# A selective scan whose gate y*silu(z) is made by VectorE out of PSUM, with five shared products a chunk in place of four

## The reference

```python
def step(h, inp):                       # over the 1024 tokens of a sequence
    ut, dt_, bt, ct = inp
    dA = jnp.exp(dt_[..., None] * A)
    dBu = ((dt_ * ut).reshape(b, nCh, ch, 1) * bt[:, :, None, :]).reshape(b, din, ds)
    h = dA * h + dBu
    y = (h.reshape(b, nCh, ch, ds) * ct[:, :, None, :]).sum(-1).reshape(b, din)
    return (h, y)
...
y = ys.transpose(1, 0, 2)
y = (y + u * D) * jax.nn.silu(z)
return y @ Wout.T + bout
```

## Time and profile before

| | |
|---|---|
| median of 3 runs | 901.68 us (898.56 to 904.07) |
| profiled execution | 903.63 us |
| its span, first to last instruction | 901.8 us |
| busy: PE, DVE, POOL, ACT | 738.7, 642.1, 512.7, 322.8 us |
| mean granted TensorE clock | 0.934 |

### The profile page before, as it was taken

One profiled execution on the slowest core, in us unless ns is written; L12 is line 12 of the kernel. 1 busy time (PEld: TensorE's weight loads), 2 busy tenths in 40 slices (PEclk: granted clock), 3 DMA queues, 4 the chain that ended last, 5 costly groups with the idle time before them and its releaser, 6 DMA issues.

```text
span 901.8 us, 10200 instructions
## 1 busy us (share of the span) xinstructions
PE 738.7 (82%) x2240; PEld 364.4 (40%) x2241; DVE 642.1 (71%) x876; ACT 322.8 (36%) x359; POOL 512.7 (57%) x266
## 2 busy tenths in 40 slices
PE   5899896878777787879678787895179999999994
PEld 3434342323232232323222232584136666666663
DVE  4467687999999999999989799486324444444442
ACT  1567675444353544444344344111021111111110
POOL 0013232889989999999988899546502222222222
PEclk9899997999999999999999899997579999999998
DMA  9354525454545554454556555296312222222220
GB/s 273 95 135 140 175 116 177 162 189 170 184 168 162 188 170 183 174 176 172 154 181 204 188 196 197 95 365 212 128 39 42 42 44 46 46 45 42 40 37 0
DMA packets 59059, 125.19 MB, mean 139 GB/s; under 512 B 9818, under 2 KB 30618, under 8 KB 58908
## 3 DMA queue, kind: packets, MB, share of 16 engines
q1 hardware_dynamic: 48676, 116.12, 39.6%
q0 software_dynamic: 7152, 8.48, 5.5%
q10 hardware_dynamic: 3208, 0.34, 0.3%
HBM read 98.01 MB, written 23.63 MB: 135 GB/s over the span
## 4 chain that ended last, share of the span: by engine, by line
PE 48%; DMA 14%; DVE 13%; POOL 9%; issue 8%; ACT 4%; another core or an unknown queue 1%; SPq 1%; ACTq 0%; DVEq 0%; POOLq 0%
PE PS L685 15%; DMA hT<-C_scratch 12%; PE PS L480 10%; DVE pool L1074 9%; PE PS L701 7%; PE PS L579 7%; POOL pool L1334 7%; ACT PS L842 2%; PE PS L595 2%; PE PS L693 2%; PE PS L561 1%; PE PS L634 1%; POOL spread L1354 1%; PE PS L673 1%
## 5 line engine op out<-in xcount | busy, mean ns | idle before, releaser
L1334 POOL TENSOR_TENSOR pool<-pool,hT 128x1024 f32<-128x1024 f32 x128 | 298.8, 2353 | 36.7 <-PE PS L579 21.8
L579 PE MATMUL PS<-pool,ident 128*128 128x512 f32 x512 | 263.1, 639 | 48.9 <-POOL pool L1334 48.1
L1074 DVE TENSOR_TENSOR_SCAN pool<-PS,pool 128x1024 f32<-128x1024 f32 x96 | 215.7, 2274 | 0.6 <-ACT PS L842 0.6
L842 ACT ACTIVATE PS<-pool,negA 128x1024 f32 (+1 forms) x128 | 143.1, 1118 | 197.1 <-DVE pool L1074 197.1
L1396 POOL DMA_INDIRECT out<-uT,ptab x39 | 60.6, 1553 | 182.9 <-DVE uT L1280 180.9
L579 PEld LDWEIGHTS PS<-pool,ident 128*128 128x128 f32 x512 | 96.5, 199 | 159.8 <-POOL pool L1334 80.8
L685 PE MATMUL PS<-pool,uT 128*128 x312 | 142.4, 600 | 0.8 <-ACT uT L899 0.4
L1062 DVE TENSOR_TENSOR pool<-PS,pool 128x1024 f32<-128x1024 f32 x96 | 117.6, 1225 | 19.2 <-ACTq L836 4.8
L561 PE MATMUL PS<-pool 96*128 96x512 bf16 x256 | 80.5, 397 | 44.3 <-DVE pool L1062 42.5
L1254 DVE TENSOR_TENSOR uT<-uT,PS 128x512 f32<-128x512 f32 x39 | 26.8, 688 | 90.3 <-PE PS L685 87.6
L1354 POOL TENSOR_TENSOR spread<-spread,pool 128x1024 f32<-128x1024 f32 x32 | 75.4, 2356 | 17.4 <-ACT spread L848 17.4
(11 more groups left out here) (165 smaller groups left out, 703.3 us busy)
## 6 DMA issues: line engine op xcount, KB each, us to landing
hT<-C_scratch SPq DMA_DIRECT2D x128, 512.0 KB
pool<-in_w SPq DMA_DIRECT2D x16, 512.0 KB, 10.1
uT<-expert_in_scratch SPq DMA_DIRECT2D x39, 130.5 KB, 2.0
Y<-Y SPq DMA_DIRECT2D x32, 128.0 KB, 2.4
C_scratch<-Y SPq DMA_DIRECT2D x8, 512.0 KB, 2.6
pool<-du_scratch SPq DMA_DIRECT2D x8, 512.0 KB, 10.9
Y<-in_wo SPq DMA_DIRECT2D x8, 512.0 KB
x_tok<-in_x SPq DMA_DIRECT2D x4, 512.0 KB, 8.8
```

The source lines that it names most:

```text
L579: m = pe.matmul(PS[:, 6 + half, :], ident[:, :], prod[:, k % PR, HF * half:HF * half + HF], start=False, stop=k == DS - 1)
L842: act.activation(pair(2 * (k % 2)).unsqueeze(1), delta[:, bass.ds(g2 * 2 + r, 1), :], ACT.Exp, scale=decay[:, bass.ds(g2 * (2 * DS) + n, 1 ...
L1074: dve.tensor_tensor_scan(hst[:, k % HR, :], pair(2 * (k % 2)), driven, 0.0, ALU.mult, ALU.add).then_inc(scan_done, 1)
L1334: gp.tensor_tensor(prod[:, k % PR, :], hst[:, k % HR, :], crep[:, k % RC, :], ALU.mult).then_inc(prod_done, 1)
```

## The change

The gate moves to VectorE, which multiplies the sum in PSUM by silu(z) and writes `uT` in one instruction, behind scan(2) of the next chunk. ScalarE's copy and GpSimd's product go. The semaphore `yev_done`, which frees banks 6 and 7, now counts gates; `gated` goes. `SHARED` has five states a chunk instead of four, so VectorE makes 11 drives a chunk and GpSimd five shared products. The loop over chunks starts at the first pair on ScalarE and GpSimd; on VectorE the first pair is written out now, since only its first chunk has no gate. The parity of `dbu` counts across the two chunks of a pair, as 11 is odd.

```diff
-SHARED = (2, 6, 10, 14)
+SHARED = (2, 5, 8, 11, 14)
...
@@ SyncE
-            sp.wait_ge(gated, NG)
+            sp.wait_ge(yev_done, 1 + NG)
...
@@ TensorE, outward_y
-                    pe.wait_ge(gated, CH)
+                    pe.wait_ge(yev_done, 1 + CH)
...
-                    pe.wait_ge(gated, CH * NB)
+                    pe.wait_ge(yev_done, 1 + CH * NB)
...
@@ ScalarE
-            def leave(g2, r):
-
-                act.wait_ge(ysum_done, g2 * (2 * DS) + ((r + 1) * DS + RC))
-                act.sem_inc(passed, 1)
-                act.activation(uT[:, bass.ds(g2 * 2 + r, 1), :], pair(6).unsqueeze(1),
-                               ACT.Copy).then_inc(yev_done, 1)
...
-                        if k == LAG - 1 and not (first and r == 0):
-                            leave(g2 - (1 - r), 1 - r)
-
-            decays_of(0, True)
-            with act.Fori(1, NG // 2) as g2:
-                decays_of(g2, False)
-            leave(NG // 2 - 1, 1)
+
+            with act.Fori(0, NG // 2) as g2:
+                decays_of(g2)
...
@@ VectorE
+            def gate_y(g2, r):
+                chunk = bass.ds(g2 * 2 + r, 1)
+                dve.wait_ge(ysum_done, g2 * (2 * DS) + ((r + 1) * DS + RC))
+                dve.tensor_tensor(uT[:, chunk, :], pair(6).unsqueeze(1), szT[:, chunk, :], ALU.mult).then_inc(yev_done, 1)
+
-            def driven_of(g2, last):
+            def driven_of(g2, first, last):
                 for r in range(2):
                     for k in range(1, DS):
                         if k not in SHARED:
                             drive(g2, r, k)
                         scan(g2, r, k - 1)
+                        if k == LAG - 1 and not (first and r == 0):
+                            gate_y(g2 - (1 - r), 1 - r)
                     if r == 0 or not last:
                         drive(g2 + r, 1 - r, 0)
                     scan(g2, r, DS - 1)
...
-            def gate_y(c):
-                dve.wait_ge(yev_done, 1 + c + 1)
-                dve.tensor_tensor(uT[:, c, :], uT[:, c, :], szT[:, c, :], ALU.mult).then_inc(gated, 1)
-
...
             residual(0)
-            gate_y(NG - 1)
+            gate_y(NG // 2 - 1, 1)
...
@@ GpSimd
-            def gate_y(g2, r):
-                chunk = bass.ds(g2 * 2 + r, 1)
-                gp.wait_ge(yev_done, g2 * 2 + (r + 2))
-                gp.sem_inc(passed, 1)
-                gp.tensor_tensor(uT[:, chunk, :], uT[:, chunk, :], szT[:, chunk, :], ALU.mult).then_inc(gated, 1)
-
...
-                        if k == RC + 2 and not (first and r == 0):
-                            gate_y(g2 - (1 - r), 1 - r)
```

More of the change, by code:

```diff
@@ L240, in adaln_mamba_moe @@
         d_done, zero_rows, xs_zeroed, z_mm, sz_done = (sem(n) for n in ("d_done", "zero_rows", "xs_zeroed", "z_mm", "sz_done"))
-        folded, gated, bout_done = (sem(n) for n in ("folded", "gated", "bout_done"))
+        folded, bout_done = sem("folded"), sem("bout_done")
         regated = sem("regated")
@@ L860, in skip, with decays_of @@
                 act.activation(chunk, chunk, ACT.Copy, scale=Dcol[:, bass.ds(g2 * 2 + r, 1)]).then_inc(ud_done, 1)
-            def decays_of(g2, first):
+            def decays_of(g2):
                 for r in range(2):
@@ L1061, in drive @@
                 dve.wait_ge(scan_done, g2 * (2 * DS) + (n + 1))
-                dve.tensor_tensor(dbu[:, owned_to(k) % 2, :], pair(4), du[:, r, :], ALU.mult).then_inc(dbu_done, 1)
+                dve.tensor_tensor(dbu[:, (r * OWN + owned_to(k)) % 2, :], pair(4), du[:, r, :], ALU.mult).then_inc(dbu_done, 1)
             def scan(g2, r, k):
@@ L1070, in scan @@
                 else:
-                    driven = dbu[:, owned_to(k) % 2, :]
+                    driven = dbu[:, (r * OWN + owned_to(k)) % 2, :]
                     dve.wait_ge(dbu_done, g2 * (2 * OWN) + (r * OWN + owned_to(k) + 2))
@@ L1087, in _ @@
             drive(0, 0, 0)
-            with dve.Fori(0, NG // 2 - 1) as g2:
-                driven_of(g2, False)
-            driven_of(NG // 2 - 1, True)
+            driven_of(0, True, False)
+            with dve.Fori(1, NG // 2 - 1) as g2:
+                driven_of(g2, False, False)
+            driven_of(NG // 2 - 1, False, True)
             route = [0]
@@ L1334, in weigh, with weighed_of @@
                 gp.tensor_tensor(prod[:, k % PR, :], hst[:, k % HR, :], crep[:, k % RC, :], ALU.mult).then_inc(prod_done, 1)
-            def gate_y(g2, r):
-                chunk = bass.ds(g2 * 2 + r, 1)
-                gp.wait_ge(yev_done, g2 * 2 + (r + 2))
-                gp.sem_inc(passed, 1)
-                gp.tensor_tensor(uT[:, chunk, :], uT[:, chunk, :], szT[:, chunk, :], ALU.mult).then_inc(gated, 1)
-            def weighed_of(g2, first):
+            def weighed_of(g2):
                 for r in range(2):
@@ L1356, in _ @@
             gp.sem_inc(ysum_done, RC)
-            weighed_of(0, True)
-            with gp.Fori(1, NG // 2) as g2:
-                weighed_of(g2, False)
+            with gp.Fori(0, NG // 2) as g2:
+                weighed_of(g2)
             gp.wait_ge(ysum_done, RC + NG * DS)
```

## The result

| | before | changed kernel |
|---|---|---|
| median | 902.88 us (898.56 to 904.08, 4 runs) | 938.43 us (929.83 to 941.48, 4 runs) |
| ratio, 95% interval | | 1.0408 (1.0357 to 1.046) |
| profiled execution, span | 903.63, 901.8 us | 937.42, 935.6 us |
| mean granted TensorE clock | 0.934 | 0.910 |

What follows compares the result with a forecast made beforehand. VectorE and GpSimd, both near their limit in the scan, form a ring through TensorE. Drives and gates -2.7, hand-over +15.7, old waits -13.0, rows of C +8.0 sum to +8.0 us: 910 us, range 898 to 917.

Steps and rivals of the forecast that it cites:

- the place: Sign of being right: VectorE waits some 1.9 us at scan(5) for shared product S5; GpSimd idles 4 us before w2.
- -2.7: VectorE in the scan: eight drives fewer, -10.7 us, and seven gates more, +8.0 us.
- The ring's floor: VectorE and GpSimd, waiting on each other through TensorE, need at least 52.8 us a chunk instead of 50.96.
- w2 starts 4.02 us after 368.6: Hand-over of y: weighing of state 2 follows the gate's end by the old copy-to-w2 time, at 372.6 instead of 369.93.
- 13.3 us in seven chunks: VectorE at scan(5) waits 1.9 us a chunk for shared product S5, delayed behind w2.
- the forecast's +8.0: Sum for the whole kernel: -2.7 + 15.7 - 13.0 + 8.0 us.
- The rival with the low clock: Hand-over meets TensorE's lower clock in two of seven chunks at 2.5 us, C's waits at upper bound: 919 us; chance 0.13.
- 13.0 us of old waits: VectorE's earlier waits for products, B's rows and its own scans, replaced by the new floor: -13.0 us.
- 8.0 for rows of C: GpSimd's 13.5 us of waits for C, most often at w11, stay and partly reach VectorE: +8 us.
- the forecast's lower bound: For rows of C: 0 us, if the longer pause at w2 lets the transfers catch up.
- the locked stretch: From S5 to S14 GpSimd (9.24 us per three steps) and VectorE (9.22) run locked.

Runs made afterwards that it cites:

- the gate alone: The changed kernel with the four shared products of before (states 2, 6, 10, 14), so only the gate is moved; 932.66 us, ratio 1.0441.
- five shared products alone: The kernel before with shared products at states 2, 5, 8, 11, 14, ScalarE's copy and GpSimd's gate kept; 912.15 us, ratio 1.0171.
- front(4) repeated: The changed kernel with the matmuls that spread B of state 4 issued four times over, ahead of u*D; 919.82 us, ratio 1.0326.
- all five fronts: The changed kernel with the B matmuls of states 0, 4, 7, 10 and 13 issued four times over; 914.84 us, ratio 1.0196.
- copy behind exp(4): The kernel before with ScalarE's copy of y one state later, behind exp(4) instead of exp(3); 941.48 us, no ratio computed.
- copy stays: The changed kernel with ScalarE's copy of y put back; VectorE gates behind scan(2) from the copy in SBUF; 904.11 us, ratio 1.01.
- the kernel with the copy, the gate behind drive(4) and its fronts filled: The changed kernel with ScalarE's copy kept, VectorE's gate from SBUF behind drive(4), B matmuls of states 0, 7, 10, 13 issued four times; 898.38 us, ratio 0.9983.

## Why the prediction was wrong

**What held.** The direction; the place, w2 and S5 on GpSimd, drive(6) and scan(5) on VectorE; the gate's 1.20 us, never held and never waiting for its sum. The drives are 88 and the scans 128, for -2.7. The ring's floor held where TensorE keeps its clock: gate to w2 5.21 against 5.24 us, VectorE's wait 1.99 against 1.9, 53.1 us a chunk against 52.8.

**The step that failed** is "w2 starts 4.02 us after 368.6" in the part on the hand-over. It took u*D and back(0) from the earlier trace rows, 1.98 and 1.88 us, and moved them back by the delay as they stood. But those rows follow an idle time of 0.34 us, and the move made it 2.80. At the lower level of TensorE's clock they take 3.78 and 2.99, w2 comes 2.84 us later still, and the wait that was put at 13.3 us in seven chunks is 30.7. That makes 17.4 of the 30 us by which the scan's +38.0 goes beyond the forecast's +8.0. The Trainium skill (TensorE: Matmul & The Clock Gate, Part 1) says that an idle TensorE loses half its clock until it has been busy again; the rows agree, 0.50 granted from 382 to 386 us.

The rival with the low clock named this mechanism and was given 0.13, at two chunks of seven by 2.5 us. The size per chunk was close (2.84 at w2); the count was wrong. "About an eighth of the time is low" was an average over the scan, and I used it as a chance that a hand-over meets a low clock. The chunks don't draw it by lot: each has the same pause at the same place, and the clock fell in all seven of the changed kernel and in six of seven with the gate behind scan(1).

**The old waits and the C rows.** The forecast took 13.0 us of old waits off and put 8.0 for rows of C on. GpSimd's waits for C are 7.1 us, not 13.5, nearer the forecast's lower bound. That the longer pause at w2 did this, as that bound supposed, isn't shown: the gate alone has the same pause and waits 22.3 us for C in 20 places (150 to 600 us), five shared products alone have the old pause and wait 6.2. In their place stand more falls of the clock, as at back(6), which hold w8 for 1.49 us and reach VectorE at scan(11), since the locked stretch has no room. These are worth most of the other 12 us of the 30, by the profiled executions: from the first drive to the last gate the changed kernel takes 476.7 us, with front(4) repeated 462.5, with all five fronts 448.6. So 14.3 go with the clock at the hand-over and 13.8 with it elsewhere, 28.1 of the 30; two executions of the changed kernel differ by 3.0 in this (476.7 and 473.7). By the whole span the second step is worth 6 us (918.4 to 912.3) and by the ratios 12 (1.0326 to 1.0196); the two kernels ran on different chips.

**What is settled and what isn't.** Shown: a delay of the hand-over alone brings such a loss (copy behind exp(4), a longer delay than the change's); taking the delay away brings 3% back (copy stays); keeping TensorE's clock up brings 21 us of the 36 back without touching the delay (by the whole time; in the scan of the profiled executions on that chip 25.1, 473.7 to 448.6). Open: what the kernel with filled fronts still loses. In the scan of the profiled execution it is 9.9 us, near the forecast's +8.0; by its ratio, 1.0196, it is some 18 (11 to 25). The kernel before isn't free of falls (0.94 over its scan) and this one nearly is (0.98), so some of the 28.1 may be falls that were there before the change, and the ring by itself may cost more than 9.9. Nor was it found why the five shared products alone cost 1.7%, or why the kernel with the copy, the gate behind drive(4) and its fronts filled isn't clearly faster than before, though it has 11 drives a chunk instead of 12. The locked stretch would explain both, as a floor that both kernels share, but no run tells that apart.

## What to carry to other kernels

When a step moves on a chain that passes through TensorE, look at the idle time that the move opens in front of its matmuls before taking their durations over (u*D took 1.98 us behind a pause of 0.3 and up to 3.78 behind 2.8), and price it in every period in which the same pause comes back, not as a chance. Look at the queue's order along with the producer's place: moving the gate alone exchanged one pause for another (1.0245), and moving the matmul as well took the loss away (0.9977).

## What the runs showed of the hardware

- Idle time directly ahead doesn't by itself tell whether the clock has fallen. back(6) of the changed kernel took 3.60 us after 1.56 us idle, and u*D with the repeated front 1.98 after 1.50, at a granted clock of 1.00. What the engine did before differs: eight front matmuls in 1.90 us ahead of the second, two in 0.60 us ahead of the first.
- Repeated matmuls with no use, 1.90 us instead of 0.60 for front(4), made the whole faster, in places where TensorE had been idle, since the matmuls behind them ran at the full clock.
- A VectorE product with both inputs in SBUF was held by a running GpSimd product: 2.04 to 3.40 us instead of 1.20. The same product with one input in PSUM took 1.20 us in every chunk, beside the same weighings. The Trainium skill (SBUF — State Buffer, the section on the two separate sides) says that such an operation and a GpSimd one take the port pair in turn for a whole instruction, and the rows agree: the gate ended 1.1 us behind w1. What it costs the total isn't shown: with most of the holding gone the ratio is 1.0131, with it 1.01, but the granted clock over the scan differs as well (0.91 and 0.96).
- The kernel before took 886 to 917 us in the runs of one chip, and by the runs that the ratios use its medians on three chips were 892.7, 892.1 and 903.6. One per cent is only seen against runs from the same chip and rounds.
